# A graph layer with residual and layer norm: the bias of 38 row pairs added by VectorE in place of a TensorE product

## What is computed

```
hx  = einsum('ni,rio->rno', x, weight)            # 8 relations
agg = segment_sum(hx[edge_type, src], dst)        # 12500 messages
y   = agg * sqrt(0.5) + h_bias + (x @ loop_weight) * sqrt(0.5)
out = layernorm(x + y)                            # over the 256 features, eps 1e-5
```

## Time and profile before

| what | value |
|---|---|
| median of 3 runs | 748.49 us (746.54 to 748.69) |
| the profiled execution | 746.04 us, of which 743.8 us from the first to the last instruction |
| PE busy | 637.3 us (86%) |
| DVE, ACT, POOL busy | 555.1 (75%), 476.6 (64%), 507.3 (68%) |

### The profile page before, as it was taken

One profiled execution on the slowest core, in us unless ns is written; L12 is line 12 of the kernel. 1 busy time (PEld: TensorE's weight loads), 2 busy tenths in 40 slices (PEclk: granted clock), 3 DMA queues, 4 the chain that ended last, 5 costly groups with the idle time before them and its releaser, 6 DMA issues. The chain is left out here.

```text
span 743.8 us, 15650 instructions
## 1 busy us (share of the span) xinstructions
PE 637.3 (86%) x4510; PEld 567.8 (76%) x4510; DVE 555.1 (75%) x1825; ACT 476.6 (64%) x1140; POOL 507.3 (68%) x496
## 2 busy tenths in 40 slices
PE   1899686999999999999999999999999999999430
PEld 1767466998888889988999998888888788888210
DVE  4999659666767676655555799999999898898540
ACT  1799724466666767555656567777777767777620
POOL 6999927677777777777774704767666776676273
PEclk9999988999999999999999999999999999999755
DMA  4733134799898887777786698999999999997421
GB/s 141 242 114 114 57 99 148 243 320 317 303 306 279 314 299 254 248 251 216 259 244 208 212 300 277 297 317 323 330 329 319 320 317 342 341 318 241 140 88 42
DMA packets 69953, 182.68 MB, mean 246 GB/s; under 512 B 12730, under 2 KB 28512, under 8 KB 69871
## 3 DMA queue, kind: packets, MB, share of 16 engines
q1 hardware_dynamic: 50287, 134.44, 53.8%
q0 software_dynamic: 19584, 47.23, 20.1%
HBM read 104.98 MB, written 82.97 MB: 253 GB/s over the span
## 5 line engine op out<-in xcount | busy, mean ns | idle before, releaser
L787 DVE TENSOR_TENSOR xt_low<-xt_ps,xt_high 128x512 fp32r<-128x512 f32 x231 | 158.2, 685 | 101.6 <-ACT xt_high L1011 100.1
L1184 PE MATMUL y_ps<-w_high,xt_high 128*128 128x256 f32 x712 | 202.2, 284 | 0.0
L1184 PE MATMUL y_ps<-w_low,xt_high 128*128 128x256 f32 x712 | 201.9, 284 | 0.0
L1184 PE MATMUL y_ps<-w_high,xt_low 128*128 128x256 f32 x712 | 201.8, 283 | 0.0
L1011 ACT ACTIVATE xt_high<-xt_ps 128x512 fp32r<-128x512 f32 x231 | 135.9, 588 | 45.8 <-PE xt_ps L1152 45.6
L595 POOL DMA_INDIRECT out_rows<-y_fix,fix_at x99 | 98.9, 999 | 77.8 <-ACT y_fix L1083 57.3
L1049 ACT ACTIVATE y_out<-y_ps,rstd 128x256 f32<-128x256 f32 x356 | 146.9, 466 | 0.1
L566 POOL DMA_INDIRECT gathered<-in_x,src_at x105 | 110.5, 1053 | 46.8 <-issue 29.6
L1184 PEld LDWEIGHTS y_ps<-w_high,xt_low 128*128 128x128 f32 x712 | 136.3, 191 | 7.9
L573 POOL DMA_INDIRECT message_rows<-message_out,edge_at x105 | 106.3, 1012 | 49.1 <-issue 29.6
L1152 PE MATMUL xt_ps<-ident,x_in 128*128 128x128 f32 (+1 forms) x784 | 119.9, 276 | 20.8 <-DMA x_in<-in_x 16.1
(11 more groups left out here) (166 smaller groups left out, 1051.5 us busy)
## 6 DMA issues: line engine op xcount, KB each, us to landing
x_in<-in_x SPq DMA_DIRECT2D x97, 512.0 KB, 5.3
out_rows<-y_out SPq DMA_DIRECT2D x97, 512.0 KB
message_in<-message_rows SPq DMA_DIRECT2D x99, 128.0 KB, 7.4
keys<-key_table SPq DMA_DIRECT2D x12, 512.0 KB, 7.4
column_of<-out_rows SPq DMA_DIRECT2D x9, 512.0 KB, 6.8
out_rows<-column_of SPq DMA_DIRECT2D x9, 512.0 KB, 3.7
w_rel<-in_L_gnn_weight SPq DMA_DIRECT2D x1, 2048.0 KB, 14.5
gathered<-in_x,src_at POOLq DMA_INDIRECT x105
```

What stands on the lines that cost most here:

```text
L787: nc.vector.tensor_tensor(xt_low[:, q % XT_RING, :], xt_ps[q % 2][:, :], xt_high[:, q % XT_RING, :].bitcast(F32), ALU.subtract).then_inc(l ...
L1184: return nc.tensor.matmul(to, xt[:, at_row:at_row + P], w, start=start, stop=stop)
```

## The change

The bias product of 38 main pairs is left out: of the second pair of each "m m" in the message stage, whose next slot is a message slot (numbers 23, 25, ... 97). Their first of the 12 products opens the accumulation. DVE adds the bias instead, in place in PSUM, over both tiles of the pair in one instruction, behind the residual `low(s+2)` and ahead of the pair's bn_stats, which wait for it. All of these pairs end a block. Nothing else changes.

```diff
+        BIAS_BY_DVE = [n for n in sorted(m_at) if g_at[0] < m_at[n] < g_at[MPAIRS - 1] and at_slot(m_at[n] + 1)[0] == "g"]
+        bias_number = {n: i + 1 for i, n in enumerate(BIAS_BY_DVE)}
...
+            def add_bias(m):
+                if m not in bias_number:
+                    return
+                dve.wait_ge(product, m_at[m] + 1)
+                y = y_ps[bank[m_at[m]]][:, :].rearrange("p (t d) -> p t d", t=2)
+                nc.vector.tensor_tensor(y, y, bias_b[:, :].unsqueeze(1).broadcast_to([P, 2, D]), ALU.add).then_inc(biased, 1)
...
-                dve.wait_ge(product, m_at[m] + 1)
+                if m in bias_number:
+                    dve.wait_ge(biased, bias_number[m])
+                else:
+                    dve.wait_ge(product, m_at[m] + 1)
...
                 low(s + 2)
+                if kind_before == "m" and s > HOLD:
+                    add_bias(before)
...
-                if kind == "m":
+                alone = kind == "g" or n in bias_number
+                if not alone:
                     nc.tensor.matmul(y_ps[bank[q]][:, :], ones_r[:, :], bias_rows[:, :], start=True, stop=False)
...
-                        first, end = kind == "g" and k == 0, k == KT - 1 and (kind == "g" or t == 1)
+                        first, end = alone and k == 0, k == KT - 1 and (alone or t == 1)
```

More of the change, by code:

```diff
@@ L343, in gnn_layernorm_kernel @@
         masks_built = sem("masks_built")
+        biased = sem("biased")
         edge_key_ready = sem("edge_key_ready")
@@ L346, in gnn_layernorm_kernel, with at_slot @@
         chunk_used = sem("chunk_used")
+        def at_slot(s):
+            return slots[s] if 0 <= s < len(slots) else ("-", None, ())
+        BIAS_BY_DVE = [n for n in sorted(m_at) if g_at[0] < m_at[n] < g_at[MPAIRS - 1] and at_slot(m_at[n] + 1)[0] == "g"]
+        bias_number = {n: i + 1 for i, n in enumerate(BIAS_BY_DVE)}
         def wait(eng, s, value):
@@ L394, in f_tile @@
             return y_ps[4 + i % 2][:, 0:D]
-        def at_slot(s):
-            return slots[s] if 0 <= s < len(slots) else ("-", None, ())
         PART = R * KT * D // 8
@@ L1164, in multiply @@
             def multiply(q, offsets):
-                kind = slots[q][0]
+                kind, n, _ = slots[q]
                 held = q < HOLD
```

## The result

The changed kernel takes 761.36 us (median of 4 runs, 759.87 to 762.11) against 747.51 us of the kernel before on the same chip (with a fourth run; the first three had a median of 748.49): ratio 1.0195, 95% interval 1.0163 to 1.0227, or 14 us slower. Its profiled execution has a span of 759.9 us.

The account below looks back on a forecast made before the run. A chain over DVE and ACT was taken to end together with PE's work; -3.2, +10.1 and +3.0 us gave +9.9, with held blocks +12 on 746.0, 758.0; the median's 2.4 more made 760.4, stated as 760, range 751 to 768.

Parts of the forecast that it names:

- Chain and PE end together in single message groups: Message stage: PE's own work and a chain over DVE and ACT reach the next message slot's first product at the same moment.
- PE's saving, 0.23 us a slot: Main slots losing the bias product: 0.23 us net in 38 slots, 8.7 us if PE alone set the pace.
- The add, 0.72 us on the chain: DVE, between residual and bn_stats: 0.69 us duration plus 0.03 until bn_stats start; bounds 0.64 and 0.86.
- Kind 1: 14 intervals starting with a double message group: chain stays covered, PE's gain counts, -0.23 us each, -3.2 us.
- Kind 2: 14 intervals starting with a single group behind a double one: the whole 0.72 us shows, +10.1 us.
- Kind 3: 10 intervals starting with a single group behind a single one: the DVE and ACT loop adds 0.30 us each, +3.0 us.
- The held blocks: Nine blocks between slots 33 and 95 with extra bn_stats and aggregate on DVE: less is covered, +2 us, maybe 0 to 5.
- Signs: What would show it: ACT's wait up 0.7 us, single-behind-single slots 0.5 to 0.8 us idle, message stage 10 to 14 us longer.
- PE as the only bound: Rival: loads or chain have slack, all 38 slots keep 0.23 us, -8.7 us, 739.8 us; chance 0.06.
- the dearer add: Rival: add at 0.86 us or more, with delays carrying among held blocks, +18.2 us, 767 us; chance 0.17.
- the clock: Rival: longer waits return PE to its lower clock for a tenth of the stage, some 15 us more, 775; chance 0.03.
- The register loads: PE's two loads before a message slot's first product: last link of the chain, starting 0.17 us behind the residual.

Follow-up runs that it names:

- e1: Kernel before with the bias product left out of the 38 pairs and no add in its place; ratio 0.9952 to the kernel before.
- e2: Kernel before with its bias products kept, plus a DVE add of zeros behind the residual; ratio 1.0234 to the kernel before.
- e3: The change with the add ahead of the residual in DVE's order instead of behind it; ratio 1.0086 to the kernel before.
- e4: The kernel of e1 profiled once more, one execution; message stage from slot 26 to 151 4.2 us shorter than in the kernel before.
- e8: The change with PE's two register loads of a message pair issued one slot earlier; ratio 1.0121 to the kernel before.
- e7: Kernel before with PE's two register loads of a message pair issued one slot earlier; ratio 0.9868 to the kernel before.

## Why the prediction was right, point by point

Forecast 760, range 751 to 768, slower; measured 761.4.

- *Chain and PE end together in single message groups:* shown. e1 keeps about half of PE's saving, e2 shows the add's cost whole, e3 removes two thirds of the loss by a swap. From slot 96 on, the first product of a single message slot behind a single one comes 1.21 us behind its transposes, from 0.41.
- *PE's saving, 0.23 us a slot:* 31 of the 38 slots take 1.87 or 1.88 us, from 2.10; the other seven, all before slot 96, are longer (up to 2.32).
- *The add, 0.72 us on the chain:* 0.79. The duration was right (0.690), the instruction behind it starts 0.10 us after its end, not 0.03.
- *The 38 intervals by kind* (first product to first product, after less before, read off PE's rows): the 14 behind a double group came to +2.5 us (I had -3.2), the 14 behind a first single one to +5.7 (+10.1), the 10 behind a second single one to +5.4 (+3.0). Together 13.5 against 9.9 and 2 for the held blocks. In two executions of one kernel (e1 and e4) the sum of a kind differs by up to 1.3 us, most of it before slot 96, so the three misses are larger than that spread. They cancel, and that the measured time came within 1.4 us of the forecast is in part luck. Kind 1 is the one that failed: I took the chain for covered behind double groups, with 0.45 us to spare where it grows by 0.79. From slot 96 on it breaks even (-0.04 on average), since the first product of the single slot behind it comes 0.14 us later than before; among the held blocks it loses. Kind 2 is smaller by about that: where kind 1 pushes the group's first product out, less is left for the next interval (from slot 96 on 0.79 - 0.14 = 0.65, measured 0.57). Kind 3, which I had put at 0.30 by the loop over DVE and ACT, would be 0.37 with an add of 0.79, and came to 0.42 from slot 96 on.
- *The held blocks:* 8.7 of the 13.5 us lie in the 22 intervals that start before slot 96, 4.9 in the 16 others. By my sum they would be 7.7 and 4.1. e3's remaining loss lies there too, so the place behind the residual is not all of it; I have not tried a kernel without held blocks, so how much is theirs, and by which wait, stays open.
- *Signs:* the stage came out just above the 10 to 14 us that I had named, ACT's wait 0.8 longer in place of 0.7. That single slots behind double groups would start as before is where it failed: 0.14 us later from slot 96 on, 0.58 among the held blocks.
- *Rivals:* PE as the only bound is refuted by e1 and e2; the dearer add by its duration; the clock by 1.00 throughout the stage. The register loads, which I had drawn as the chain's last link, are refuted as the cause by e8.
- *The Trainium skill's rule* of free semaphores (VectorE: DVE Perf Modes, "The DRAIN you can't avoid") does not carry over to an instruction that waits for the one before it on its own engine: the residual and e3's add, each followed by an instruction that does not wait for them, are followed after 0.61 and 0.60 us, the change's add, for which bn_stats wait, after 0.79 (357.28 to 358.07), all of the same size.

## What to carry to other kernels

An engine that is free for a third of the time can still be the one that everybody waits for: before work is moved to it, follow one period in order of time and ask between which two links the new instruction falls. Put it where its engine waits for somebody else anyway; one slot earlier the same add showed no cost, and one instruction up in the same queue it left a third of the loss. And when an engine's idle time is zero by coincidence of two lengths, taking work off it gives back only part (here 4.6 of 8.7 us), and lengthening the other costs only part (16.4 us of 38 times 0.79, which is 30): count for each period which of the two ends last.

## What I had not expected of the hardware

An addition that writes PSUM in place took 0.690 us at 128x512 and 0.423 at 128x256, the same as the residual that writes SBUF (0.69); but the waiting instruction behind it started 0.10 us after its end, against 0.03 behind bn_stats that write SBUF. With no wait behind it (e3) the next one started 0.09 us ahead of its end, about as behind the residual. And the register loads of PE's sequencer: between 0.29 and 1.15 us each, for four bytes. Issued one slot early (e7), they no longer held up the second slot of a double group, and the stage was 12.5 us shorter.
